# Unread TensorE products in three waits of a two-layer decoder: the ends of the cross attention, the sparse layer and the delta rule

## The reference, cut to what matters

```python
def _layernorm(x, axis=-1, eps=1e-05):
    m = jnp.mean(x, axis=axis, keepdims=True)
    v = jnp.var(x, axis=axis, keepdims=True)
    return (x - m) / jnp.sqrt(v + eps)
...
def _L0_xattn_ref(p, k_v, W_k, b_k, ln_gamma, ln_beta):      # the cross attention
    kv = k_v @ W_k.T + b_k
    out = jnp.einsum('bij,bjd->bid', p, kv)
    sim = jnp.einsum('bid,bjd->bij', out, kv) * scale
    mu = jnp.mean(sim, axis=-1, keepdims=True)
    var = jnp.var(sim, axis=-1, keepdims=True)
    sim = (sim - mu) * jax.lax.rsqrt(var + EPS) * ln_gamma + ln_beta
    return jax.nn.softmax(sim, axis=-1)
...
# the sparse layer (_L0_ffn_ref): 64 experts, 6 per token, and a shared one
router_logits = x @ gate_w
topk_w, topk_ids = _grouped_topk(router_logits, bias)
y = _routed_moe(x, topk_w, topk_ids, w_gate, w_up, w_down)
shared = jax.nn.silu(x @ ws_gate) * (x @ ws_up) @ ws_down
...
# the delta rule (_L1_attn_ref), per head:
S = S * jnp.exp(gt)
delta = (vt - kt @ S) * bt
S = S + kt[:, None] * delta[None, :]
# then o normalised per head, times silu(gate), times Wo
...
x = _layernorm(x + _L0_xattn_ref(x, ctx_512, ...), axis=-1)
x = _layernorm(x + _L0_ffn_ref(x, ...), axis=-1)
x = _layernorm(x + _L1_attn_ref(x, ...), axis=-1)
```

## Time and profile before

| | |
|---|---|
| time, median of 3 runs | 1410.56 us |
| lowest and highest | 1408.77 and 1411.58 us |
| the profiled execution's own time | 1410.06 us |
| its span, first to last instruction | 1408.1 us |
| around the span | 1.96 us |
| TensorE busy | 1274.9 us (91%) |
| VectorE, ScalarE, GpSimd busy | 812.5, 547.8, 522.8 us |
| mean granted TensorE clock | 0.932 |

### The profile page before, as it was taken

The page is one execution under the profiler, slowest core; times in us unless marked ns, Lnnn a source line. Parts: engine busy times, 40 slices in busy tenths (PEclk is TensorE's granted clock), DMA queues, the critical chain, the costliest instruction groups (busy, mean ns, idle before and its releaser), DMA issues. The chain is left out here.

```text
span 1408.1 us, 25115 instructions
## 1 busy us (share of the span) xinstructions
PE 1274.9 (91%) x9172; PEld 843.7 (60%) x9172; DVE 812.5 (58%) x1826; ACT 547.8 (39%) x1273; POOL 522.8 (37%) x597
## 2 busy tenths in 40 slices
PE   8999999847886877999999987799999999899998
PEld 4868778635555444577777766345555555344487
DVE  5464655557345476676776423577777774743343
ACT  4554646133223476767667331043434342000000
POOL 3452636430751367476577301322222211500010
PEclk9999999958798798999999966899999999999999
DMA  3010039533896201212122120110000205542100
GB/s 131 24 37 15 22 105 279 184 143 139 235 261 199 79 11 21 45 29 42 33 37 28 19 43 1 44 38 21 21 22 21 72 1 176 176 137 70 34 8 23
DMA packets 163367, 106.57 MB, mean 76 GB/s; under 512 B 88128, under 2 KB 152872, under 8 KB 162112
## 3 DMA queue, kind: packets, MB, share of 16 engines
q1 hardware_dynamic: 155104, 88.31, 22.7%
q0 software_dynamic: 4496, 13.33, 3.1%
q10 hardware_dynamic: 3664, 3.55, 0.8%
HBM read 84.16 MB, written 22.35 MB: 76 GB/s over the span
## 5 line engine op out<-in xcount | busy, mean ns | idle before, releaser
L2814 PE MATMUL la_banks<-la_xe,la_f_w 128*128 128x512 f32 x348 | 151.4, 593 | 3.5 <-DVE la_xe L3192 3.5
L2173 DVE SCALAR_TENSOR_TENSOR dh_front<-dh_pj,df_conv,dh_front 128x510 f32<-128x510 f32 x144 | 107.3, 745 | 76.2 <-ACT dh_front L1912 72.4
L3355 POOL TENSOR_TENSOR la_area<-la_area 128x512 f32<-128x512 f32 x48 | 60.3, 1278 | 174.0 <-DVE la_area L3035 153.6
L2814 PEld LDWEIGHTS la_banks<-la_xe,la_f_w 128*128 128x128 f32 x348 | 65.4, 190 | 83.7 <-issue 83.6
L346 POOL TENSOR_TENSOR wa_qkT<-lf_area 128x512 f32<-128x512 f32 x40 | 50.8, 1270 | 97.6 <-DVE lf_area L318 97.6
L3192 DVE TENSOR_TENSOR la_xe<-xT,la_area 128x1024 f32<-128x1024 f32 x29 | 52.6, 1830 | 54.0 <-PE la_banks L2814 48.2
L2932 ACT ACTIVATE la_area<-la_banks,la_nmax 128x256 f32<-128x256 f32 x128 | 58.9, 474 | 58.5 <-DVE la_nmax L3044 58.5
L350 POOL TENSOR_TENSOR mw_gu<-mw_gu,const 128x384 f32<-128x384 f32 x64 | 63.7, 1001 | 29.9 <-ACT mw_gu L381 29.9
L3375 POOL TENSOR_TENSOR la_o_rstd<-la_o_var,la_minus_half 128x1 f32<-128x1 f32 x8 | 6.4, 803 | 164.3 <-DVE la_o_var L3254 164.3
L2940 ACT COPY la_area<-la_banks 128x512 f32<-128x512 f32 x64 | 37.5, 589 | 56.3 <-PE la_banks L2663 56.0
L273 PE MATMUL wa_po<-wa_wo,mw_rows 128*128 128x256 f32 x256 | 56.6, 379 | 0.0
(11 more groups left out here) (621 smaller groups left out, 3092.0 us busy)
## 6 DMA issues: line engine op xcount, KB each, us to landing
placed<-mw_rows SPq DMA_DIRECT2D x8, 768.0 KB, 10.4
mw_gu<-in_L_ffn_w_gate SPq DMA_DIRECT2D x16, 384.0 KB, 7.3
mw_gu<-in_L_ffn_w_up SPq DMA_DIRECT2D x16, 384.0 KB, 10.6
mw_d<-in_L_ffn_w_down SPq DMA_DIRECT2D x16, 384.0 KB, 9.5
mw_rows<-placed SPq DMA_DIRECT2D x8, 768.0 KB, 6.6
la_area<-w_table POOLq DMA_DIRECT2D x6, 1024.0 KB, 11.9
pairs<-me_picked SPq DMA_DIRECT2D x7, 704.0 KB, 4.0
la_f_w<-in_L_ffn_q_proj SPq DMA_DIRECT2D x32, 128.0 KB, 2.2
```

Of the source, the lines that this page charges most:

```text
L2173: dve.scalar_tensor_tensor(dst, src[:, :, 0:SEQ - j], conv[:, a, m, D_CONV - 1 - j:D_CONV - j], dst, ALU.mult, ALU.add).then_inc(tapped, 1)
L2814: mm = pe.matmul(acc[c][m], f_w[n % SLOTS][:, m, k, :], xe[(n - U) % RING][:, k, :], start=first and k == 0, stop=last and k == KC - 1)
L3355: pool.tensor_tensor(qrot[:, c, n, :], prod[:, c, 2 * n, :], prod[:, c, 2 * n + 1, :], ALU.add).then_inc(rotated, 1)
```

## The change

Three places get matmuls whose result nothing reads. Each multiplies the identity by a part of `env.xT` that is complete and isn't being written, into a bank whose contents are no longer wanted.

- Cross attention: after the wait for `l_copied` and a new wait for `added` of 4, five products of 128 x 512, before the transposes.
- Sparse layer: after the row sums of tile 7, five products of 128 x 256, with no wait of their own, before `turn_x(1)`.
- Delta rule: after waits for `og_copied` of 4 and `added` of 4, five products of 128 x 512 before `turn_last`; and after `out_last` and a wait for `og_copied` of 6, four more before `turn_normed`.

```diff
@@ cross_with_norms, tensor
                 mm.then_inc(mo_done, 1)
                 pe.wait_ge(l_copied, 2)
+                pe.wait_ge(added, 4)
+                for n in range(5):
+                    pe.matmul(kp[:, 0, :], env.c("ident"), env.xT[:, 0, 0:512], start=True, stop=True)
                 for th in range(2):
                     for kc in range(KC):
                         turn(tile2_ready, (kp, kt)[th][:, kc, :], turned2, th, kc)
@@ routed_experts, tensor
                         turn_x(0)
+                for n in range(5):
+                    pe.matmul(op[:, 0, 0:DIM], env.c("ident"), env.xT[:, 0, 512:512 + DIM], start=True, stop=True)
                 turn_x(1)
@@ delta_attention, tensor
+                def spin(count):
+                    for n in range(count):
+                        pe.matmul(tp[:, 0, :], env.c("ident"), env.xT[:, 0, 0:512], start=True, stop=True)
+
+                pe.wait_ge(og_copied, 4)
+                pe.wait_ge(added, 4)
+                spin(5)
                 for f in range(2):
                     turn_last(f)
                 for f in range(2):
                     out_last(f)
+                pe.wait_ge(og_copied, 6)
+                spin(4)
                 for th in range(2):
                     turn_normed(th)
```

## The result

| | before | after |
|---|---|---|
| median of 6 executions each, on one chip | 1410.35 us | 1417.3 us |
| lowest and highest | 1408.77 and 1413.87 | 1414.41 and 1421.26 |
| the profiled execution's own time | 1410.06 | 1416.55 |
| its span | 1408.1 | 1414.5 |
| mean granted TensorE clock | 0.932 | 0.939 |

The ratio is 1.005 (95% interval 1.0034 to 1.0066). The change makes the kernel 0.5% slower, although TensorE's mean clock went up. I had forecast 1411.4 us, in a range up to 1415.0. (One execution of the kernel before on chip 9 took 2774.2 us at a mean clock of 0.47; the ratios of that chip leave it out.)

What follows compares the result with a forecast made beforehand. Three stage ends, each one chain in which TensorE waits for a layer norm, were taken to bound the kernel. 1410.06 + 3.3 - 0.5 - 1.5 - 0.2 = 1411.2, given as 1411.4 us for the median, range 1407.8 to 1415.0.

Steps and rivals of the forecast that it cites:

- What bounds the kernel: Three stage ends are single chains in which TensorE waits for a layer norm; a microsecond there is one of the whole.
- Price of a product: A 128 x 512 product costs 1.75 us at half clock, 0.86 us at full; five cost 8.7 or 4.3 us.
- Cross attention, +3.3: Five products start cold at 297.1 with 1.8 us of room and delay the transposes; net loss 3.3 us.
- Sparse layer, -0.5: The group costs nothing and keeps the clock up through the transposes; gain 0.5 us, bounds -0.7 and 0.
- Delta rule, first group, -1.5: Five products before the outputs hold the clock, so VectorE's first addition comes earlier; gain 1.5 us, bounds -1.9 and 0.
- second, -0.2: Delta rule's second group costs 0 to 0.3 us and speeds the following transposes; gain 0.2 us, next stage cold.
- The sum: 1410.06 + 3.3 - 0.5 - 1.5 - 0.2 = 1411.2 us against the profiled execution; 1411.4 given for the median.
- Rival 1: Cross attention group stays cold (+6.9 us); second condition: it costs 3.3 to 4.2 with a loss behind; 1415 us, chance 0.14.
- Rival 2: The clock is carried into one of the three next stages, shortening its cold start; 1407 us, chance 0.09.
- Rival 3: Products ahead of the transposes cost nothing, being short or passed by ready transposes; 1407.2 us, chance 0.03.
- Rival 4: Products don't hold the clock in the last two stages, leaving the cross attention's +3.3 alone; 1413.4 us, chance 0.13.
- The range: Whole kernel: 1407.8 to 1415.0 us, taking in all the forecast's bounds and the edges of the rivals.

Runs made afterwards that it cites:

- e1_cross: Only the change's five products at the cross attention's end, added to the kernel before; 1412.41 us, ratio 1.0021.
- e11_all_third: The whole change, measured a third time against the kernel before; 1416.58 us, ratio 1.0041.
- e3: Only the two groups at the delta rule's end (five and four products), added to the kernel before; 1407.64 us, ratio 0.9991.
- e13: The change without its cross attention group (sparse and delta groups), a second time, against the kernel before; 1421.79 us, ratio 0.9995.
- e14: Only the two delta rule groups, a second time on another chip, against the kernel before; 1418.69 us, ratio 0.9987.
- e12: Only the first delta rule group, ahead of `turn_last`, added to the kernel before; 1410.47 us, ratio 1.0009.
- the early whole: The whole change with seven cross attention products placed ahead of the wait for `l_copied`, against the kernel before; 1422.16 us, ratio 0.9980.
- e17: All groups, the cross one early, plus products behind the last transposes of all three ends (one, three, one), against the kernel before; 1408.63 us, ratio 0.9919.
- e15_cross_delta: The change without its sparse group (cross attention and delta groups), against the kernel before; 1424.80 us, ratio 1.0026.

## Why the prediction was wrong, step by step

**What bounds the kernel.** The places were right, and so was the reading that a microsecond in them is one of the whole, except at the sparse layer's end. There I read the chain through the last transpose and the barrier and took it that the barrier waits for the transposes. A barrier of 2.88 us before L1626 beside one of 2.55 before L865 and 2.47 before L2616 was the hint that this one had something else in it.

**Price of a product.** Right: ten records took 7.46 us with a rise after 5.9 (8.7 cold), 4.54 at full clock.

**Cross attention, +3.3 (bounds +2.7 to +4.2).** Right in its queue, start (forecast 297.1, measured 297.43) and size. The group ended at 304.7, the late edge of 303.1 to 304.6. Over five traces with this group of five the router was late by 4.26, 2.75, 3.22, 2.78 and 4.37 us, mean 3.5. As forecast the router started cold in three of them, the change's own among them. In the other two, e1_cross and e11_all_third, the clock was still at 1.00 for the router's first 1.2 us, the products took 5.93 us, and VectorE's wait for the logits ended only 1.6 us late; over the five it ended 3.0 us late. Measured as time, the group alone gives +2.8 (0.9).

**Sparse layer, -0.5.** The transposes gained the 0.55 us of the forecast. The step that failed is the wait behind the transposes: I let the barrier follow them, and it takes the 0.55 us back in full (8.24 us from the last row sum to the next stage, 8.23 before). The term is 0.

**Delta rule, first group, -1.5, and second, -0.2.** The groups lie where they should and the gain in this stage is there: over nine traces with both groups the stretch is 16.98 us on average against 18.18 in six without them, -1.2 for a forecast of -1.7. The forecast holds where the clock held under the outputs: in e3, e13 and e14 the stretch is 16.4 to 16.6 us, and in e12, without the second group, 16.75, so the second group's 0.2 fits too. In the other six of the nine the clock dipped there, and the stretch is 17.01 to 17.63. Over all fourteen kernels with a delta group it held in four of the five without a cross attention group and in none of the nine with one, the whole change included. No run shows why. In the change's own trace the first addition came only 3.46 us after the first transpose, against 3.90 before, since the clock dipped at 883.6, under the outputs: the loss I had named as possible and given to "some executions"; it is in all three traces of the whole change. The start of the last stage gained besides, which I had not forecast: it began at 1.00, where I had it cold (12.89 us on average over the nine, 13.63 over the six: -0.74; but two of the six, with no delta group, have 12.65 and 12.67). The step that failed is the one that wasn't made: I closed the account at L2616. The last stage was 1.5 us longer, with a second dip of the clock (501.7 on average over the nine, 500.2 over the six). In sum of the traces the groups are worth -0.5 us; measured, -1.7 (0.8).

**Around the span.** I took the 1.96 us around the span as fixed. It is 1.9 to 2.0 us on average in the kernel before and in every experiment, but 2.40, 2.66 and 2.52 in the three comparisons of the whole change (26 executions, up to 3.5 us in one). Cross with delta has 1.93, the early whole 1.97. So 0.6 us of the loss is outside the span, and in the measured kernels only where all the groups stand together with the cross one at the late place. I have no cause for it.

**The sum.** With what the runs showed it is +3.5, 0, -0.5 and +0.6, thus +3.6 us, where I had forecast +1.1. (The three traces of the whole change alone give the same: +3.0 at the wait for the logits, 0, 0.0 for the delta groups and +0.6.) So the steps that failed are the two credits and the fixed time around the span: of -0.5 and -1.7 us the traces show 0 and -0.5, or 0.0 in the change itself, and the 1.96 us around the span became 2.5. The prediction also adds wrongly at its end: 1411.2 and the 0.5 us named there make 1411.7, not 1411.4; that changes nothing here. The whole change measured +5.3 (0.8). Some 1.7 us remain unexplained, about two standard errors. They are not in one place of the traces, and cross with delta (+3.3, 0.9) doesn't show them. Whether it is an interplay of the groups or the spread stays open.

**The rivals.** Rival 1 had the time nearest to the measured one (1415 against 1417.3; its bounds went to 1418), and its second condition was met: the cross attention cost 4.26 us in the profiled execution with losses behind it. Its first was not: the group didn't stay cold, in any of the five traces. Rival 2, the clock carried into the next stages, happened in part: at L2630 in the change (at 1.00 for its first 0.6 us, one of the signs I had named for being wrong), at the router in e1 and e11, not at L1631 in the change. In full it is what tail products bring about in e17. Rival 3 is refuted by the 5.46 us for which VectorE waited: transposes that are ready don't pass the products ahead of them, and a record took 430 ns at full clock. So the sentence of the Trainium skill, page "TensorE: Matmul & The Clock Gate", section "Step-by-step: what each phase is for", that matmuls stay in program order, holds here by that number. Rival 4, at +3.3 us and 1413.4, is the nearest to the account of the runs, by luck: its reason, that the products don't hold the clock, is wrong for the sparse layer and in part for the delta rule. They do hold it there, and earn next to nothing in time in the whole change.

**The range.** It was built from the terms, and left out that the median of six executions of this kernel moves by itself. Executions of the kernel before on chip 6 lie between 1404 and 1419 us. The standard error of a comparison was 0.8 to 1.7 us.

## What to carry to other kernels

A filler belongs where its engine has nothing to wait for and where it is over before the real work is ready: place it by the wait that stands ahead of it in the engine's list, not by the first moment at which the engine is idle. Such products cost 3 us behind a late wait and brought some 3 us at an earlier point. The fastest kernel, measured once, also has them behind the last real work of each stage, where they carry the clock into the first products of the next; how much of its gain is theirs is open. Before a shorter tail is counted as a gain, look whether the barrier behind it keeps its distance to an earlier event, and follow the account to the end of the program.

## What the runs showed of the hardware that I had not expected

- After a cold start, with products of 128 x 512 without a pause, the granted clock rose after 2.9 to 6.1 us in five traces of the same group (2.9 in e1_cross, 5.9 in the change, 6.1 in e15_cross_delta). The price of the same ten records went from 5.97 to 7.58 us with it.
- A barrier can have a floor that TensorE's work doesn't set: at the sparse layer's end the next stage starts 5.64 us after GpSimd's last power in 19 of 20 traces, with the last transpose 0.56 us earlier or not. The distance is shown, its cause isn't.
- One program, executed again on one chip, spreads over 10 us and more, and stretches of its trace by up to 4 us, and with it moves where short dips of the clock fall; the last stage is about 1.5 us longer for each dip near 1165 or 1230 us (498.7, 500.1, 501.7).
- A higher mean clock says nothing of the time. The change raised it from 0.932 to 0.939 and was slower; e17 has 0.953 and is faster.
